# Extra bf16 products on TensorE while a mixture stage works out its first routing weights

## What is computed

```python
h = gelu(unfold(x) @ tok_weight + tok_bias)            # 128 x 82 x 64
h = h + relu_attention(layernorm(h))                   # causal, relu instead of softmax
h = h + mixture0(layernorm(h))                         # 6 experts of 3 layers, top 2
h = h + rope_attention(layernorm(h))                   # causal softmax with rotary parts
n = layernorm(h)
h = h + n + sum_e combine[:, e] * expert_e(n)          # 8 experts of 2 layers, top 2
```

## Time and profile before

| | value |
|---|---|
| median of three runs | 764.93 us |
| the profiled execution: its time | 765.2 us |
| the profiled execution: span from first to last instruction | 763.3 us |
| TensorE busy | 667.6 us (87%) |
| VectorE busy | 508.5 us (67%) |
| ScalarE busy | 312.5 us (41%) |
| GpSimd busy | 188.1 us (25%) |
| mean granted TensorE clock | 0.916 of full speed |

### The profile page before, as it was taken

The page is one execution under the profiler, slowest core; times in us unless marked ns, Lnnn a source line. Parts: engine busy times, 40 slices in busy tenths (PEclk is TensorE's granted clock), DMA queues, the critical chain, the costliest instruction groups (busy, mean ns, idle before and its releaser), DMA issues. The chain is left out here.

```text
span 763.3 us, 15616 instructions
## 1 busy us (share of the span) xinstructions
PE 667.6 (87%) x5903; PEld 422.5 (55%) x5903; DVE 508.5 (67%) x1515; ACT 312.5 (41%) x707; POOL 188.1 (25%) x200
## 2 busy tenths in 40 slices
PE   3599999979995899999997977999864989999995
PEld 2575665569983444555553456888663434444432
DVE  3546889458682376766577449999874576677783
ACT  0010101134432457566564527576551353444442
POOL 1000000355533101222003036788253203221000
PEclk9799999989995799999998998999865697999998
DMA  9967962000000000000000000000000000000001
GB/s 299 412 224 257 322 239 109 2 0 2 1 3 0 1 0 2 2 0 1 1 1 1 1 0 2 1 3 1 2 1 0 1 18 11 19 19 18 19 19 27
DMA packets 28122, 38.94 MB, mean 51 GB/s; under 512 B 19344, under 2 KB 19600, under 8 KB 28048
## 3 DMA queue, kind: packets, MB, share of 16 engines
q1 hardware_dynamic: 19232, 35.46, 13.0%
q10 hardware_dynamic: 8816, 2.49, 1.6%
HBM read 35.25 MB, written 2.69 MB: 50 GB/s over the span
## 5 line engine op out<-in xcount | busy, mean ns | idle before, releaser
L419 POOL TENSOR_TENSOR centred<-h,mean 82x512 f32<-82x512 f32 x64 | 66.5, 1040 | 435.0 <-DVE rstd L408 260.4
L1490 DVE TENSOR_TENSOR m_hm<-bank,m_h 128x656 f32<-128x656 f32 x112 | 93.7, 837 | 71.5 <-PE bank L1322 48.9
L280 PE MATMUL bank<-cols,tok_weight 64*64 64x328 f32 (+1 forms) x2200 | 120.5, 383 | 23.6 <-issue 11.7
L1218 ACT ACTIVATE m_h<-bank,m_b 128x656 f32<-128x656 f32 x112 | 90.3, 806 | 121.6 <-PE bank L1313 121.6
L280 PEld LDWEIGHTS bank<-cols,tok_weight 64*64 64x64 f32 x2200 | 78.5, 151 | 62.5 <-issue 13.2
L1313 PE MATMUL bank<-m_xt,m_w 64*128 64x328 f32 x448 | 98.3, 517 | 4.2 <-ACT m_h L1218 3.3
L1338 PE MATMUL bank<-m_hm,m_wo 128*64 128x328 f32 x448 | 95.8, 477 | 1.1 <-DVE m_hm L1490 1.1
L317 DVE COPY cols<-image 128x1992 f32<-128x1992 f32 x32 | 62.1, 1958 | 29.2 <-DMA image<-in_x_dram 15.1
L1313 PEld LDWEIGHTS bank<-m_xt,m_w 64*128 64x128 f32 x448 | 35.8, 196 | 60.5 <-issue 40.5
L421 POOL TENSOR_TENSOR xn<-centred,rstd 82x512 f32<-82x512 f32 x64 | 66.6, 1041 | 5.0
L1330 PE MATMUL bank<-m_h,m_w 128*128 128x328 f32 x192 | 66.6, 470 | 0.0
(11 more groups left out here) (167 smaller groups left out, 1106.3 us busy)
## 6 DMA issues: line engine op xcount, KB each, us to landing
image<-in_x_dram SPq DMA_DIRECT2D x32, 1000.0 KB, 9.7
out_dram<-m_fin SPq DMA_DIRECT2D x16, 164.0 KB
tok_weight<-in_L_tok_weight_dram ACTq DMA_DIRECT2D x2, 400.0 KB, 8.6
m_w<-in_L_ffn_w_dram ACTq DMA_DIRECT2D x2, 128.0 KB
m_sel_raw<-c_sel_dram ACTq DMA_DIRECT2D x1, 256.0 KB
m_w<-in_L_ffn_expert_w_dram ACTq DMA_DIRECT2D x2, 96.0 KB
m_sel_raw<-c_sel_dram ACTq DMA_DIRECT2D x1, 192.0 KB
m_bo_raw<-in_L_ffn_expert_b_dram ACTq DMA_DIRECT2D x9, 1.5 KB
```

Source lines behind the costliest of these rows:

```text
L280: return pe.matmul(sum_bank[u % 2][s][t * D:(t + 1) * D, L * j0:L * j1], weight[s * R:(s + 1) * R, c, :], cols[u % 2][s * R:(s + 1) * R, c ...
L419: pool.tensor_tensor(self.centred[:], slots(self.h, g), mean.broadcast_to([L, G, D]), ALU.subtract).then_inc(self.shifted, 1)
L1218: act.activation(h1[n % RING][:], h1_bank, ACT.Gelu if last else ACT.Relu, bias=W.b1[:, k:k + 1]).then_inc(h1_ready, 1)
L1490: dve.tensor_tensor(hm[k][:], cb_bank, src[n % RING][:], ALU.mult).then_inc(hm_ready, 1)
```

## The change

Each mixture's TensorE stream gets products whose result nobody reads. A helper `keep_busy(n)` issues n matmuls of `ident16` (128 x 128) with the first 384 columns of `W.sel` into bank 7. Eight follow the logits of each of the three front groups. Twelve more (sixteen in the second mixture) stand right ahead of `turn_combine(0)`, in the first mixture behind the wait for the third group's logits. The products wait for nothing and signal nothing. No other engine's stream is changed, and no DMA.

```diff
+                def keep_busy(n):
+
+                    for _ in range(n):
+                        pe.matmul(psum[:, 7, 0:3 * 128], ident16[:], W.sel[:, 0:3 * 128], start=True, stop=True)
+
                 for f in range(FRONT):
                     turn(f)
                     if not last:
                         router(f)
                     logits(f)
+                    keep_busy(8)
                 if not last:
                     pe.wait_ge(lg_read, FRONT)
+                keep_busy(16 if last else 12)
                 turn_combine(0)
                 layer1(0, 0)
```

## The result

The changed kernel took 762.7 us in the median against 765.3 us of the kernel before in the same session (ratio 0.9964, 95% interval 0.9948 to 0.9981), so 2.6 us less (one of its ten executions took 1577.2 us and stays out of the ratio). A second session gave 763.6 against 765.6 us (0.9978, 0.9954 to 1.0002), an interval that just reaches 1. Weighed together that is about 2.3 us less, where 2.4 us more was forecast. It is a small gain, inside the 0.5% that this measurement resolves badly.

The account below looks back on a forecast made before the run. The prediction took TensorE as busiest, with waits on VectorE's last `cp` and half-clock work behind them setting the end. 4.0 - 2.4 + 5.2 - 4.4 = +2.4 us gave 767.6 on 765.2, 767.3 in the median; range 760.0 to 772.0.

Parts of the forecast that it names:

- One product, 0.32 cold and 0.16 warm, loads hidden: Each added 384-column product takes 0.32 us at half clock, 0.16 at full, its weight load running beside the product before.
- Rival 2: Added products' weight loads stand in the open: 0.47 us cold, 0.25 warm each; +10.9, 776 us; chance 0.12 shared with another.
- The first mixture, 4.0 late: Delayed rounds and the run of twenty make the first mixture's `turn_combine(0)` start 4.0 us late (3.6 to 4.7).
- The rise in the first mixture's run: TensorE's clock rises after 5.1 us of gapless work, the middle of 3.6 and 6.5 us, with 16 products done.
- 2.4 back: First mixture, `turn_combine(0)` to third `layer1`: 5.7 us at full clock instead of 8.1, so 2.4 us back.
- The second mixture, 5.2 late: Second mixture's `turn_combine(0)` starts 5.2 us late (4.4 to 6.5), held by its 24 products.
- 4.4 back: Second mixture, `turn_combine(0)` to fifth `layer1`: 8.3 us warm instead of 12.7, so 4.4 us back.
- Carried whole to the end: Nothing behind the two starts is edited and TensorE has little slack there, so the +2.4 us sum reaches the end whole.
- rival 1: The clock rises already in the front rounds: -5.6 us, 759.3 median for both mixtures, about 763 for one; chance 0.27.

Follow-up runs that it names:

- first_only: The change's products in the first mixture only (8 a round, then 12), against the kernel before: 763.5 against 765.3 us, 0.9982.
- run_first: First mixture only: all 20 products behind the third logits, none in the earlier rounds, against the kernel before: 759.8 against 765.6 us, 0.9932.
- run_second: Second mixture only: all 24 products behind the third logits, none in the earlier rounds, against the kernel before: 760.6 against 766.3 us, 0.9930.
- run_only: Both mixtures: all products (20 and 24) behind the third logits, none in the earlier rounds, against the kernel before: 758.2 us, 0.9903.
- first_held: Kernel before plus the change's first-mixture products and products at later waits in the second mixture's loop: 762.1 against 765.0 us, 0.9967.
- second_held: Kernel before plus the change's second-mixture products and products at later waits in that mixture's loop: 760.1 against 765.0 us, 0.9948.
- whole_held: The changed kernel plus products at later waits in the second mixture's loop, against the kernel before: 759.3 against 766.3 us, 0.9914.
- second_only: The change's products in the second mixture only (8 a round, then 16), against the kernel before: 760.9 us, 0.9945.
- gaps_held: Like run_only, plus a few products in the front rounds' short gaps and at the second mixture's later waits, against the kernel before: 753.8 against 766.3 us, 0.9833.
- thin_full: Placed as in run_only, but 60 + 90 products of 16 columns instead of 384, against the kernel before: 765.8 against 765.0 us, 1.0011.
- run_thin: Placed as in run_only, but 14 + 22 products of 16 columns instead of 384, against the kernel before: 765.2 against 765.6 us, 1.0000.

## Why the prediction was wrong

The forecast was 4.0 - 2.4 + 5.2 - 4.4 = +2.4 us. The measured time lies inside its range of 760.0 to 772.0 us, but on the other side of the kernel before. Term by term:

- **One product, 0.32 cold and 0.16 warm, loads hidden:** right. Eight take 2.72 us cold, 24 take 4.06 warm, with 0.16 and 0.22 beyond the products themselves. Rival 2 is out.
- **The first mixture, 4.0 late:** `turn_combine(0)` came 3.06 late in the first trace and 4.0 in the second (24.79 us after the first turn against 20.76). The two differ in when the clock falls at the stage's start: in the first it was still full for the first turn and router, 2.6 us into the stage. The kernel before had it fall at 0.1 us, the changed kernel's second trace at 0.5, so the 4.0 is the fairer number. A round costs 1.72, forecast 1.8.
- **The rise in the first mixture's run:** 4.9 us into it (0.63 over 250 to 255 us puts it at 253.7) and 5.6 in the second trace, forecast 5.1. The trace agrees with the rule of the Trainium skill that activity releases the half clock ("TensorE: Matmul & The Clock Gate", "Part 1: The HAM clock gate").
- **2.4 back:** 2.63 measured. The third `layer1` is 0.4 to 1.4 late, forecast 1.6. Up to the last turn of its output the whole stage took 214.0 and 214.9 us in the changed kernel and 214.5 before. So 0.9 came back behind the third `layer1`, where the kernel before has 6.8 us at half clock late in the stage (from 184.5 us after its first turn) and the changed one 3.4 us or none. The forecast stopped at the third `layer1`. So this half is worth about nothing by the traces, and -1.4 (-2.8 to +0.1) by first_only's time.
- **The second mixture, 5.2 late: the step that failed.** It took the rise to come 5.1 us into the run of 24. It came in the rounds, behind the first eight, 5.7 to 6.5 us after the first turn, in all six traces that have eight products in these rounds. So it was no luck of one execution. `turn_combine(0)` was 1.8 late, not 5.2.
- **4.4 back:** from `turn_combine(0)` to the fifth `layer1` 8.07 us, forecast 8.3, before 12.73. Right: 4.7 back. This start gains 2.9 us where +0.8 was forecast: 3.7 of the 4.7 us by which the sum was off.
- **Carried whole to the end:** wrong in size, both ways. Later dips, which the sum didn't have, move the second mixture's rest between 146 and 153 us. From the kernel before to the changed one the first mixture's stage changes by -0.5, the second's start by -2.9 and its rest by +1.6, together -1.7 us (-0.9 with the second trace), against -2.3 by the times.

The forecast had this as rival 1, with a chance of 0.27, and argued against it with a stretch of gapless work at 600 to 604.9 that had 16-column logits in it and didn't lift the clock. That was the wrong neighbour. The same stretch says more, since TensorE had worked without a gap from 595.49 on:

```profile
595.50:605.00 9.50, 9.50 (x38) 4.21 (x38) 4.27 (x10) 2.79 (x4) 2.08 (x2) 0.50 0.00 0
```

So with this one the kernel before shows rises after 3.6, 6.5 and 9.4 us of gapless work, and the 5.1 was the middle of two of them: the moment of the rise was far less certain than the terms that hang on it make it look. Nor does the length of gapless work tell the two mixtures apart. Logits, eight products and the next turn make 4.4 us without a gap in both (233.88 to 238.28 and 580.50 to 584.90). In the second mixture the rise stands near their end in each of the six traces (5.7 to 6.5 us after the first turn, where they end at 6.2); in the first none of the six with these products has a rise in the rounds. Why is open.

Rival 1 for the second mixture alone, +1.6 - 3.2 = -1.6, comes near the result. The forecast names this case ("one of them, about 763"), but gives it no chance of its own.

What stays open is why the halves don't add up: about -6 together against -2.3 whole, run_first and run_second -11.6 against run_only's -7.1, and the other way round with the later dips held off (first_held -2.9 and second_held -4.9, whole_held -7.0), where the sessions differ besides. The runs of one kernel fall in groups (second_only 755.9 to 761.5 and three at 765.7 to 767.0 with a lower clock, 0.924 to 0.926), and which groups a kernel has seems to change with every shift of its schedule. That is argued from the dips above, not shown.

## What to carry to other kernels

Work that only keeps the clock up is worth placing where TensorE waits anyway, and only there: the run alone gave 7 us, the same products with eight in each round 2.3, and a run with one or two more products in each short gap (four behind the first turn) gave 11. Size it to the wait at the clock that will then hold, since a run that turned warm ends early and leaves the gap it was to fill. And when a gain rests on the clock, look for the later waits that let it fall again: filling those in the second mixture gave 5 us by itself, and the best version here, gaps_held, is at 753.8 us against 766.3 us (0.9833).

## What the runs showed of the hardware

The Trainium skill says in "TensorE: Matmul & The Clock Gate", section "Weight-path perf modes", that 128 weights that aren't float32 load fast. Thin_full fits that: 150 products with a fresh 128 x 128 load each took 4.15 us, 0.028 us apiece at half clock, although a load's own record there is 0.104 us long. So the loads hide behind each other or are faster than their records; the trace doesn't tell which.

In one place of the first mixture two kernels show TensorE nearly always busy: thin_full 4.78 of the 5.0 us from 245 to 250, at clock 0.50 and with no rise behind it; run_only 4.83 of the same 5.0 us, with the rise 4.9 us after its run began (3.9 us in the second mixture). In the kernel before, TensorE worked for 9.4 us without a gap, from 595.49, before the clock rose.

The dips of the clock can fall at nearly the same places of the program in different executions. In the changed kernel's two traces the second mixture's events came at +6.2 and +6.0, +57.4 and +57.2, +71.0 and +70.9 us after its first turn; in the kernel before and run_thin at +26.9 or +27.0, +61.1 and +71.3 in both. They don't always: the changed kernel's first mixture went to half clock 2.6 us after its first turn in one trace and 0.5 us in the other. That a small shift of the schedule swaps one set of dips for another is argued from this, not shown.
